# GpSimd's order in the last attention pair, one bank for each tile of the last group, and one activation-table load less

## The reference

```python
# x: (32, 112, 256), ctx: (32, 375, 128), 16 heads of 64
qh = heads(layernorm(x) @ Wq); kh = heads(ctx @ Wk); vh = heads(ctx @ Wv)
attn = softmax(einsum('bhnd,bhmd->bhnm', qh, kh) * 64 ** -0.5)
x = x + tanh(g_xattn) * (merge(einsum('bhnm,bhmd->bhnd', attn, vh)) @ Wo + bo)

xf = layernorm(x).reshape(3584, 256)
gates = softmax(xf @ router_w)                   # 14 routed experts, the best 2 kept and normalised
ffn(xn, rw, W1, W2) = silu((xn * rsqrt(mean(xn * xn) + eps) * rw) @ W1) @ W2
x = x + tanh(g_ffn) * (sum over the 2 kept experts of gate * ffn(...)
                       + sum over 2 shared experts of ffn(...))
```

## Time and profile before

| | |
|---|---|
| median of the three runs | 1454.03 us |
| the profiled execution's own time | 1453.46 us |
| its span in the trace | 1451.9 us |
| PE busy | 1433.0 us, 99% of the span |
| PE weight loads | 1346.5 us, 93% |
| DVE / ACT / POOL busy | 1081.6 (74%) / 935.3 (64%) / 458.0 us (32%) |
| granted PE clock, mean | 0.998 |

### The profile page before, as it was taken

The page is one execution under the profiler, slowest core; times in us unless marked ns, Lnnn a source line. Parts: engine busy times, 40 slices in busy tenths (PEclk is TensorE's granted clock), DMA queues, the critical chain, the costliest instruction groups (busy, mean ns, idle before and its releaser), DMA issues.

```text
span 1451.9 us, 29493 instructions
## 1 busy us (share of the span) xinstructions
PE 1433.0 (99%) x9774; PEld 1346.5 (93%) x9774; DVE 1081.6 (74%) x2614; ACT 935.3 (64%) x2398; POOL 458.0 (32%) x688
## 2 busy tenths in 40 slices
PE   7999999999999999999999999998999999999998
PEld 6999999999999999999999999998789988888888
DVE  4878888888888888888798888877587544444448
ACT  6777777777777777777777777776453445454552
POOL 4313142231323313143131422326100145555520
PEclk9999999999999999999999999999999999999999
DMA  4010312303112131212303112150022356562235
GB/s 126 7 52 18 116 75 55 103 24 117 75 50 82 50 109 50 84 75 57 109 16 118 75 50 95 36 194 31 28 102 116 131 179 236 212 236 92 77 123 222
DMA packets 55794, 138.02 MB, mean 95 GB/s; under 512 B 10512, under 2 KB 38176, under 8 KB 52064
## 3 DMA queue, kind: packets, MB, share of 16 engines
q1 hardware_dynamic: 49024, 118.01, 23.6%
q0 software_dynamic: 6624, 18.13, 4.0%
HBM read 86.69 MB, written 49.43 MB: 94 GB/s over the span
## 4 chain that ended last, share of the span: by engine, by line
PE 94%; DVE 2%; issue 1%; ACT 1%; POOL 1%; DMA 1%; SPq 0%; ACTq 0%; POOLq 0%
PE bank L589 18%; PE bank L590 18%; PE bank L591 18%; PE bank L650 9%; PE bank L1720 7%; PE bank L1047 6%; PE bank L1039 5%; PE bank L1743 4%; PE bank L1747 2%; PE bank L1731 2%; PE bank L1705 1%; PE bank L1223 1%; PE bank L605 1%; DMA under_wq<-in_Wq 0%; POOL keep_w_in L1149 0%
## 5 line engine op out<-in xcount | busy, mean ns | idle before, releaser
L765 ACT ACTIVATE prob<-bank,nmax 128x375 f32<-128x375 f32 x448 | 258.8, 578 | 183.1 <-DVE nmax L874 181.1
L857 DVE TENSOR_TENSOR pT_lo<-bank,pT_hi 125x384 fp32r<-125x384 f32 x448 | 245.8, 549 | 31.6 <-ACT pT_hi L776 30.1
L874 DVE TENSOR_REDUCE nmax<-bank 128x1 f32<-128x375 f32 x448 | 240.9, 538 | 24.6 <-PE bank L591 24.1
L650 PE MATMUL bank<-keep_ident,prob 128*125 128x128 f32 x1344 | 221.3, 273 | 0.0
L776 ACT CAST pT_hi<-bank 125x384 fp32r<-125x384 f32 x448 | 212.6, 475 | 1.7 <-PE bank L650 1.7
L650 PEld LDWEIGHTS bank<-keep_ident,prob 128*125 128x125 f32 x1344 | 201.9, 187 | 5.7
L589 PE MATMUL bank<-attend_wvo_hi,zT_hi 128*112 128x256 f32 x512 | 169.6, 331 | 0.1
L589 PE MATMUL bank<-attend_kvT_hi,qp_hi 128*128 128x376 f32 x448 | 151.3, 338 | 4.6 <-ACT prob L765 4.5
L589 PE MATMUL bank<-pT_hi,kv_hi 125*128 125x448 f32 x384 | 152.9, 398 | 2.8 <-DVE zT_lo L857 1.3
L590 PE MATMUL bank<-attend_kvT_hi,qp_lo 128*128 128x376 f32 x448 | 150.2, 335 | 0.0
L591 PE MATMUL bank<-attend_kvT_lo,qp_hi 128*128 128x376 f32 x448 | 149.5, 334 | 0.0
(11 more groups left out here) (238 smaller groups left out, 3715.5 us busy)
## 6 DMA issues: line engine op xcount, KB each, us to landing
w_split<-we_split SPq DMA_DIRECT2D x14, 2048.0 KB, 7.4
keep_weights<-w_split SPq DMA_DIRECT2D x14, 2048.0 KB
we_in<-in_w SPq DMA_DIRECT2D x28, 512.0 KB, 6.1
keep_y_all<-y_rows SPq DMA_DIRECT2D x14, 512.0 KB, 8.9
kv_in<-in_ctx SPq DMA_DIRECT2D x32, 187.5 KB
h_rows<-hrow SPq DMA_DIRECT2D x32, 112.4 KB, 2.6
keep_h_in<-h_rows SPq DMA_DIRECT2D x7, 514.0 KB, 9.6
x_in<-in_x SPq DMA_DIRECT2D x16, 224.0 KB, 3.0
```

Source lines behind the costliest of these rows:

```text
L650: last = nc.tensor.transpose(turn_bank_of(s)[0:MP, c * P:(c + 1) * P], prob[:, s % NB, c * MP:(c + 1) * MP], ident[:])
L765: nc.scalar.activation(prob[:, s % NB, :], score_bank(s)[:, 0:M], ACT.Exp, bias=nmax[:, s % NB:s % NB + 1], accum_out=psum_[:, s % NB:s % ...
L857: return nc.vector.tensor_tensor(dst, src, hi.bitcast(F32), ALU.subtract)
L874: nc.vector.tensor_reduce(nmax[:, s % NB:s % NB + 1], score_bank(s)[:, 0:M], AX, ALU.max, negate=True).then_inc(max_ready, 1)
```

## The change

There are three parts.

1. In the last pair, POOL's program takes the first scaling of expert 1's `w1` (as `scale_half`) ahead of the bias, then batch 29's root, and only then the bias of batch 31 and the scaling of `w2` (`scale_rest`). The waits `scaled(...)` are each moved to a later tile.
2. Group 6 gets a bank for each of its four tiles (`alone`): banks 4, 5, 6 and 7. Since 6 and 7 held group 5, PE waits for group 5's four adds. Every tile of the last item has its own signal to DVE, and the last store is split into one of two tiles and two of one tile.
3. The table load of line 817 goes.

```diff
-            sb["scale_shared"](pool, 0, lambda: scaled(4), lambda: scaled(6))
+            sb["scale_shared"](pool, 0, lambda: scaled(6), lambda: scaled(8))
+            sb["scale_half"](pool, 1, lambda: scaled(10))
+            ln2_root(2 * p - 1)
             add_bias(p, 1)
-            sb["scale_shared"](pool, 1, lambda: scaled(8), lambda: scaled(10))
-            ln2_root(2 * p - 1)
+            sb["scale_rest"](pool, 1, lambda: scaled(14))
             pool.wait_ge(side_done, job_index(p, Q[7]) + 1)
-            sb["split_shared"](pool, 0, lambda: scaled(14), lambda: scaled(16), lambda: scaled(18))
-            sb["split_shared"](pool, 1, lambda: scaled(20), lambda: scaled(22), lambda: scaled(24))
+            sb["split_shared"](pool, 0, lambda: scaled(16), lambda: scaled(18), lambda: scaled(20))
+            sb["split_shared"](pool, 1, lambda: scaled(22), lambda: scaled(24), lambda: scaled(26))
             ln2_root(2 * p)
...
-            nc.scalar.preload_act_table_set("natural_log_exp_and_others")
             for p in range(PAIRS):
...
-def shared_output(nc, sb, hid, e, t, bank):
+def shared_output(nc, sb, hid, e, t, bank, alone=False):
+    half = 0 if alone else t % 2
...
-                                stop=e == SHARED - 1 and t % 2 == 1 and n == 11, skip_group_check=True)
+                                stop=e == SHARED - 1 and (alone or half == 1) and n == 11, skip_group_check=True)
...
+        def scale_half(pool, e, wait_first):
             pool.wait_ge(rms_landed, 16 * SHARED)
             pool.wait_ge(w_landed[e], 32)
             wait_first()
...
+        def scale_rest(pool, e, wait_second):
             wait_second()
             nc.gpsimd.tensor_scalar(w2_in[:, e], w2_in[:, e], sb["tanh_g"][:, 1:2], None, ALU.mult).then_inc(w_step, 1)
...
+        def out_bank(g, t):
+            return O_BANK[t] if g == GROUPS - 1 else O_BANK[2 * (g % 2) + t // 2]
...
-            for t in (0, 2):
-                sp.wait_ge(acc_done, 4 * (g - BEFORE) + t + 2)
-                sp.dma_start(by_group(io["out"], g)[:, t:t + 2, :], acc[:, 4 * g + t:4 * g + t + 2, :]).then_inc(out_stored, 16)
-            sp.wait_ge(out_stored, 16 * (GROUPS + 1))
+            for t, n in ((0, 2), (2, 1), (3, 1)):
+                sp.wait_ge(acc_done, 4 * (g - BEFORE) + t + n)
+                sp.dma_start(by_group(io["out"], g)[:, t:t + n, :], acc[:, 4 * g + t:4 * g + t + n, :]).then_inc(out_stored, 16)
+            sp.wait_ge(out_stored, 16 * (GROUPS + 2))
...
                 pe.wait_ge(hid_lo_ok, 4 * i + 4)
+                alone = items[i][0] == GROUPS - 1
+                if alone and e == 0:
+                    pe.wait_ge(acc_done, 4)
                 for t in range(4):
-                    last = shared_output(nc, sb, hid, e, t, O_BANK[2 * (items[i][0] % 2) + t // 2])
-                    if t % 2:
+                    last = shared_output(nc, sb, hid, e, t, out_bank(items[i][0], t), alone)
+                    if t % 2 or i == len(items) - 1:
                         last.then_inc(o_done, 1)
...
-                    dve.wait_ge(o_done, 2 * i + t // 2 + 1)
+                    dve.wait_ge(o_done, 2 * i + (t if i == len(items) - 1 else t // 2) + 1)
```

More of the change, by code:

```diff
@@ L1041, in shared_hidden @@
     return last
-def shared_output(nc, sb, hid, e, t, bank):
+def shared_output(nc, sb, hid, e, t, bank, alone=False):
+    half = 0 if alone else t % 2
     for n, (j, (h, w)) in enumerate((j, q) for j in range(4) for q in PRODUCTS):
-        last = nc.tensor.matmul(bank[:, (t % 2) * D:(t % 2 + 1) * D], hid[h][:, e, j, t * P:(t + 1) * P],
-                                sb["w2s_" + w][:, e, j, :], start=e == 0 and t % 2 == 0 and n == 0,
-                                stop=e == SHARED - 1 and t % 2 == 1 and n == 11, skip_group_check=True)
+        last = nc.tensor.matmul(bank[:, half * D:(half + 1) * D], hid[h][:, e, j, t * P:(t + 1) * P],
+                                sb["w2s_" + w][:, e, j, :], start=e == 0 and half == 0 and n == 0,
+                                stop=e == SHARED - 1 and (alone or half == 1) and n == 11, skip_group_check=True)
     return last
@@ L1142, in load_front @@
                 load_h(sp, g)
-        def scale_shared(pool, e, wait_first, wait_second):
+        def scale_half(pool, e, wait_first):
             pool.wait_ge(rms_landed, 16 * SHARED)
@@ L1150, in scale_shared @@
                                         ).then_inc(w_step, 1)
+        def scale_rest(pool, e, wait_second):
             wait_second()
             nc.gpsimd.tensor_scalar(w2_in[:, e], w2_in[:, e], sb["tanh_g"][:, 1:2], None, ALU.mult).then_inc(w_step, 1)
+        def scale_shared(pool, e, wait_first, wait_second):
+            scale_half(pool, e, wait_first)
+            scale_rest(pool, e, wait_second)
         def split_shared(pool, e, wait_hi, *wait_lo):
@@ L1354, in front @@
                   split_router=split_router, load_front=load_front, load_front_w1=load_front_w1,
-                  scale_shared=scale_shared, split_shared=split_shared)
+                  scale_shared=scale_shared, scale_half=scale_half, scale_rest=scale_rest, split_shared=split_shared)
         def vector(dve):
@@ L1910, in accumulate @@
                 for t in range(4):
-                    dve.wait_ge(o_done, 2 * i + t // 2 + 1)
+                    dve.wait_ge(o_done, 2 * i + (t if i == len(items) - 1 else t // 2) + 1)
                     dve.wait_ge(y_added, 4 * TOPK * order.index(g) + 4 + t + 1)
-                    out = O_BANK[2 * (g % 2) + t // 2][:, (t % 2) * D:(t % 2 + 1) * D]
+                    half = 0 if g == GROUPS - 1 else t % 2
+                    out = out_bank(g, t)[:, half * D:(half + 1) * D]
                     nc.vector.tensor_tensor(acc[:, 4 * g + t, :], out, acc[:, 4 * g + t, :], ALU.add).then_inc(acc_done, 1)
```

## The result

The changed kernel takes 1449.00 us (median of 6 runs, 1448.57 to 1449.35), the kernel before 1454.08 us (6 runs, 1453.72 to 1455.53). The ratio is 0.996, 95% interval 0.995 to 0.997: 5.08 us faster. Forecast were 6.46 us and 1447.6 us; the measured time lies inside the range and 1.4 us above the forecast. The profiled execution took 1449.15 us, its span is 1447.3 us.

A forecast was written before the change was run, and what follows sets the result against it. PE bounds the kernel (94% of the chain), so time is won only where it waits or runs slowly. Stall -7.31, cover +1.6, table load -0.65, end -0.1 sum to -6.46 us: 1447.6 us, range 1446.0 to 1451.2.

The forecast's parts named there:

- The stall: Last pair, scores(17) to scores(20): PE's waits behind POOL's late root, and the low clock, go; -7.31 us.
- The cover: Last pair: POOL's long instructions now run beside live steps and slow DVE; +1.6 us, between 0 and 5 us.
- rival B: Last pair: disturbed DVE instructions held for POOL's whole instruction; about 4.4 us instead of 1.6; 1450.4 us; 14%.
- The table load: ACT, ahead of the first exponential: removing the load gives back PE's wait behind it; -0.65 us.
- The end: Last outputs: later PE start and last add, against a smaller last store; -0.1 us, between -0.1 and +0.6 us.
- the smaller store: End of the program: the last store, with half the bytes, lands sooner; -0.6 us, between 0 and -0.6.
- The sum: Whole kernel: all terms together give -6.46 us, so 1447.6 us; 58%.
- C: Last pair: DVE's slack hides nearly all disturbance by POOL, 0.3 us left; 1446.3 us; 14%.
- D: Last pair: POOL late after all, through weight loads or the aggregate; half the stall stays; 1451.3 us; 8%.
- E: Last pair: the next wait replaces the old one; only the table load and the end count; 1453.3 us; 3%.
- F: Last outputs: the new 0.85 us wait puts PE on the low clock, 8.6 us more; 1456.2 us; 3%.

The follow-up runs named there:

- after: The changed kernel with all three parts, against the kernel before: 1449.00 us, ratio 0.996.
- after again: The changed kernel itself once more, unchanged, on one chip beside its variants: 1448.77 us, ratio 0.9957 to the kernel before.
- p1_order: The kernel before with part 1 alone (POOL's new order): 1447.38 us, ratio 0.9946.
- load_back: The changed kernel with the table load put back ahead of the first exponential: 1449.40 us, ratio 0.9963 to the kernel before.
- w2_first: The changed kernel with the bias of batch 31 behind expert 1's `w2` scaling instead of ahead of it: 1447.69 us, ratio 0.9954.
- w2_pieces: The changed kernel with expert 1's `w2` scaled in four instructions of 128x256 instead of one of 128x1024: 1446.71 us, ratio 0.9949.
- pieces_two_stores: w2_pieces with PE's wait for group 5's adds ahead of tile 2 and two last stores of 256 KB: 1447.42 us, ratio 0.9958.
- tail_free: The changed kernel with PE's wait for group 5's adds moved from tile 0 to tile 2 of the last group: 1449.08 us, ratio 0.9962.
- g16: The changed kernel with expert 1's `w2` scaled behind tile 16's multiplication instead of tile 14's: 1447.45 us, ratio 0.9945.

## Why the prediction was right, and where it was off

**The stall: right in mechanism, and near in size.** Forecast -7.31 us, on the premise that scores(17) to scores(20) would take as long as scores(24) to scores(27), 5.53 us. With nothing held they take 5.80 us, so against the traced 12.84 us the stall was worth 7.03 us there, and by the other two traces that have it 7.6 and 8.3 us. POOL's L516 came at 984.33 (forecast near 984), ACT's idle time went, the low clock did not appear.

**The cover: right in size, wrong in kind and place.** Forecast +1.6 us, out of graded slowdowns of four instructions, most of it at tile 12. Measured +1.60 us in both traces of after (scores(17) to scores(20), 7.40 - 5.80), all from one instruction held to the end of POOL's, at tile 16; tile 12 cost nothing. That is the mechanism of my rival B at a smaller sum. The first trace has 0.3 us more from tile 10, a price that the kernel before paid too.

What a hold costs can be read off all traces with the new order. The columns are the multiplications of tiles 10 and 16 (us), what they took above 0.42 us each, and steps 11 to 27 less the 30.23 us of the free traces:

```
                    tile 10   tile 16   above    steps 11 to 27
                                        2x0.42   less 30.23
after               0.68      2.04      1.88     1.93
after again         0.42      2.04      1.62     1.62
p1_order            0.74      0.42      0.32     0.34
load_back           1.19      0.42      0.77     0.82
w2_first            0.93      1.33      1.42     1.45
w2_pieces           0.42      0.67      0.25     0.26
pieces_two_stores   0.74      0.68      0.58     0.62
tail_free, g16      0.42      0.42      0.00     0.00
```

Each microsecond of hold at these two tiles is a microsecond of PE's time: VectorE has no slack there. `hrow`'s product (0.75 us in after, 0.14 us when alone) and tile 18's don't show in the column.

The step that failed is the sentence that takes tile 10's 0.76 us as the pattern: beside the same kind of instruction tile 16 took 0.42 us or its whole remainder, so one mild row bounds nothing, and a sum of averages came near the truth by luck. What the Trainium skill says (SBUF — State Buffer, "SBUF: two separate sides"), that the loser waits for the other's whole instruction, agrees with the 2.04 and 1.33 us, and with the splits, the bias and the casts in the table of the last section; it does not cover the 0.42 us of p1_order, load_back and tail_free beside the same instruction, nor the 0.67 us that ended before the piece did.

**The table load: right, but the bound was too tight.** Forecast -0.65, and bounded by PE's wait of that length; measured -0.79 us. From scores(0) to the third scores it is 2.29 us instead of 2.98, so 0.69 us came where the load stood and 0.1 us behind it. But it moves tile 0's multiplication into POOL's split, and in one trace of ten that took back more than it gave.

**The end: wrong sign.** Forecast -0.1, measured +0.30 us. PE came 0.88 us later behind the last hidden matmul, as forecast (0.85). The last add ended 13.31 us behind the start of that matmul instead of 12.68: +0.63 (forecast +0.51). The term that failed is the smaller store: from the last add's end to the end of the span it is 1447.3 - 1444.63 = 2.67 us instead of 2.98, so -0.3 and not -0.6 us. The landing itself came near the forecast: the very last store landed 1.9 us from its issue instead of 2.4 (the 2.3 us above are the median of two, and the other took 2.7). But the span ended 0.75 us behind that landing, and in all eight traces with three stores, instead of 0.57, as in the six with two. What fills the 0.2 us isn't shown.

**The sum.** Measured terms: -5.44 - 0.79 + 0.30 = -5.93 us, against -6.46 forecast. The -5.44 is this trace pair's: 7.03 for the stall less 1.60 for the hold. The remaining 0.85 us to the medians' -5.08 lie outside the change's terms. The two profiled executions differ by +1.09 us up to scores(0) and by +0.24 us in the middle, and these stretches vary as much between kernels with the same code there. That their mean over many runs is the same with and without the change isn't shown.

**The rivals.** C (slack hides all) has the number of the executions that are free and not their mechanism: tile 16's multiplication was not hidden there, it was not held, and where tiles 10 and 16 were held, slack hid none of it; only `hrow`'s and tile 18's holds stayed hidden. D and E fell with ACT's idle time. F fell: the clock behind the waits of 1.73 and 0.72 us stayed at the high level.

## What to carry to other kernels

When a stall is removed, look for the long GpSimd instructions that it had covered, and set each where no VectorE multiplication from and to SBUF comes due beside it, or cut it in pieces. Beside a GpSimd instruction with two inputs, count the whole remainder; beside a one-input scaling, the price of one meeting went from 0 to 1.6 us with hundredths of a microsecond in the start, so give it as values with chances and not as a mean. A wait that vanishes from the list of TensorE is worth only what the next engine allows: at the end VectorE's adds and SyncE's issues were as late as TensorE. And a store that is split pays for one more issue on SyncE (0.64 us for the third one in tail_free) and for a later end behind the last landing (0.2 us).

## What the runs showed of the hardware

The hold of VectorE by GpSimd, for multiplications of 128x375 beside POOL's 128x1024 scaling of `w2` in one instruction (offset of the start, then duration; 0.42 us is the time alone):

```
expert 1's w2, held:  1.03 -> 2.04 (twice); 1.73 -> 1.33
expert 1's w2, free:  1.00, 1.01, 1.02 -> 0.42
expert 0's w2:        0.14 -> 1.19; 0.39 -> 0.93; 0.57 -> 0.76; 0.58 -> 0.74 (twice); 0.59 -> 0.74; 0.63 -> 0.68; 0.66 -> 0.66
                      0.98, 1.06, 1.07, 1.18, 1.28 -> 0.42
```

Starts within the first 0.7 us all end about 1.3 us into the scaling (0.14 + 1.19, 0.66 + 0.66); later ones are free or end 0.21 us behind it. What decides between them, some hundredths of a microsecond apart and with exceptions (1.18 and 1.28 free, 1.73 held), stays open.

This wavering belongs to POOL's one-input scalings. Here are all multiplications of 128x375 that start within a long instruction of POOL, over the 14 traces and the whole span:

```
POOL's instruction            times  outcome
two inputs, 128x1024 (split)  254    235 end 0.21 us behind it, after up to 2.18 us;
                                     the other 19 start in its last 0.3 us
two inputs, 112x256 (bias)    14     all end 0.21 us behind it
cast, 128x1024                8      all end 0.21 us behind it
scaling, 128x512              216    start 0.98 or later: 197 end 0.21 to 0.25 us
                                     behind it, 3 start in its last 0.15 us
                                     start 0.11 to 0.41: 5, all end 0.90 us into it
                                     start 0.45 to 0.83: 11, all 0.42 to 0.44 us
```

So a hold to the end is the rule beside the first three kinds (the 1.58 us of the earlier trace rows is one of them), and the scalings are where a multiplication can slip through or be let go early.

Halving the last store from 256 to 128 KB brought its own landing from 2.4 to 1.9 us where the adds were spread out. In tail_free, where the three stores were issued back to back, it was 2.4 us.
